# Two attentions in pairs of heads: another order of scores, minima and value projection, and a mixture product in banks of its own

## The chip, the cores and the metric

The kernel runs on one core of a Trainium2 chip. The metric is the device time of one execution in microseconds (us); of several executions the median counts. Five engines work side by side, each through its own instructions in order: TensorE (PE, with PEld for its weight loads), VectorE (DVE), ScalarE (ACT), GpSimd (POOL) and SyncE (SP), which here starts the DMAs. They wait for one another by semaphores.

## The reference, cut to what matters

The program is a chain of eight networks on 256 rows of 768 numbers. The change touches the first feed-forward network (`L0_ffn`, in the kernel `f0`) and the last one (`L3_ffn`, in the kernel `f3`). Both have an attention of 12 heads of width 64 over the 256 rows.

```python
# L0_ffn: x is (1, 256, 768)
normed = _ln(hidden_states, g1, b1)
scores = sigmoid(einsum('bld,d->bl', normed, Wr) + br)
_, idx = top_k(-scores, k)                      # k = 38 rows
attn_mask = zeros((b, l), bool).at[..., idx].set(True)
q, kk, v = (normed @ W + bias for q, k, v), 12 heads of 64
probs = softmax(einsum('blhd,bmhd->bhlm', q, kk) / sqrt(64), axis=-1)
attn_out = einsum('bhlm,bmhd->blhd', probs, v).reshape(b, l, d) @ Wo + bo
pooled = einsum('bl,bld->bd', scores / (sum(scores) + 1e-6), normed)
mix_out = (normed + scores[..., None] * pooled[:, None, :]) @ Wm + bm
merged = where(attn_mask[..., None], attn_out, mix_out)
h = hidden_states + merged                      # then a layer norm and a small gelu network

# L3_ffn: queries, keys and values with a low-rank part, then the same attention
attn = softmax(einsum('bhqd,bhkd->bhqk', q, k) * scale, axis=-1)
out = einsum('bhqk,bhkd->bhqd', attn, v) @ W_proj.T + b_proj
```

## The kernel before

Products are made at the precision of float32 by three products each: every weight tile of 128x768 is split by ScalarE into an upper part `WH` (line 294, `feed_act`) and by VectorE into a lower part `WL` (line 301, `feed_vec`), and activations are split the same way (lines 481 and 485: `act_upper`, `vec_lower`). There are four slots for split tiles, so `ahead(t)` feeds up to four tiles past t, and a slot is free when TensorE has done the product of the tile that held it. Each engine's program is written out by hand; no scheduler moves anything.

The attention goes by six pairs of heads, i = 0 to 5. `pair_scores` makes the scores of a pair (eight matmul records, line 358) in PSUM banks 0 and 1 or 2 and 3. VectorE takes their minima (the query is scaled by a negative number, so the minimum stands for the maximum) in `pair_least`, line 1367. ScalarE makes the exponentials with their row sums in `pair_exp`, line 1336. TensorE turns the exponentials (`turn_p`, eight transposes, line 363); ScalarE copies one half out of PSUM and VectorE the other (lines 474 and 477). VectorE makes the reciprocals of the row sums (line 1386) and, in the first network, multiplies them by the attention mask (line 1389); TensorE spreads them as rows (`spread`, line 1303). `mix` (line 1315) multiplies by the values in bank 6, `ctx` (line 1378) scales the result, and `upper` and `lower` split it for the output product.

Before: the minima of pair i+2 are the last step but one in VectorE's round i, behind the reciprocals, the lower part of pair i-2 and the copy; on TensorE the scores of pair i+2 come behind transposes and spreading of pair i. The whole value projection comes ahead of the loop.

In the first network the mixture's input `mixT` is masked on GpSimd (`l0ffn_pool`, line 1674) by a row that TensorE makes from the mask, and its lower part is made there too (line 1676). Behind the loop the mixture product and the attention's output product are summed in the same banks, for three blocks of 256 columns: each takes two tiles of one weight and then two of the other.

## Time and profile before

| | us |
|---|---|
| median of 3 runs | 1440.65 (1436.98 to 1444.83) |
| the profiled execution | 1440.82 |
| its span | 1439.0 |
| TensorE busy | 1347.7 |
| VectorE busy | 971.6 |
| ScalarE busy | 774.6 |
| GpSimd busy | 207.2 |

The span is the time from the first to the last recorded instruction; what the profiled execution took more, 1.8 us, lies around it. The engines overlap, so busy times don't add up to the span. The first network's part that matters lies from 547 to 624 us, the last network's from 1380 to 1435. In a timeline a row is a run of alike instructions with its start, its length, and in brackets how long the engine was idle before it and who ended that. PEclk is the granted share of TensorE's full clock (2.4 GHz; half of it is 1.2 GHz).

### The profile page before, as it was taken

To read this page: it belongs to the slowest core of one execution; us is meant where nothing else is said; L and a number is where in the kernel's file an instruction comes from. 1 tells how busy PE (TensorE), PEld (TensorE's weight loads), DVE (VectorE), ACT (ScalarE), POOL (GpSimd) and SP (SyncE) were. 2 spreads that over 40 slices of the span, in tenths; PEclk is the share of its full clock that TensorE was granted. 3 is DMA by queue.
4 is the path that set the end of the run, shared out by engine and by line. 5 is a ranking of instruction groups with operands and counts; after the bars stand their busy time and mean duration, and the time that the engine had idled before them with its cause. 6 is when DMAs were issued, how large, how long until landed. Compare 5 with 4: busy or idle time off the path is not lost.

```text
span 1439.0 us, 24211 instructions
## 1 busy us (share of the span) xinstructions
PE 1347.7 (94%) x10108; PEld 1157.6 (80%) x10108; DVE 971.6 (68%) x1708; ACT 774.6 (54%) x1260; POOL 207.2 (14%) x103
## 2 busy tenths in 40 slices
PE   9999999999999799888799999789999999998898
PEld 8999533799633588687688999769899999987786
DVE  8745777745777767566677767776677767768454
ACT  3445888545788545454545554634445544436344
POOL 0110776100677200002001000001000000000100
PEclk9999999999999999999899999899999999999899
DMA  9456364135464213035233453064355555232200
GB/s 355 111 201 189 100 181 121 67 132 170 128 197 121 76 68 121 1 139 202 99 136 142 171 180 132 23 242 132 134 187 176 169 194 192 73 152 102 77 1 23
DMA packets 30836, 194.82 MB, mean 135 GB/s; under 512 B 4212, under 2 KB 4340, under 8 KB 14727
## 3 DMA queue, kind: packets, MB, share of 16 engines
q1 hardware_dynamic: 30726, 193.27, 39.6%
q8 instruction: 80, 1.31, 0.4%
q14 instruction: 30, 0.24, 0.1%
HBM read 183.03 MB, written 3.93 MB: 130 GB/s over the span
## 4 chain that ended last, share of the span: by engine, by line
PE 73%; DVE 15%; ACT 7%; POOL 3%; issue 2%; DMA 0%; DVEq 0%; SPq 0%; ACTq 0%
PE PS L358 56%; PE PS L978 6%; PE PS L987 5%; DVE WL L301 3%; PE PS L363 3%; POOL WK L1173 2%; PE PS L619 1%; PE PS L460 1%; POOL WL L308 1%; DVE WK L1790 1%; ACT WK L1765 1%; ACT WH L294 1%; DVE WK L1795 1%; ACT WK L1336 1%; DVE SM L535 1%
## 5 line engine op out<-in xcount | busy, mean ns | idle before, releaser
L301 DVE TENSOR_TENSOR WL<-w,WH 128x768 fp32r<-128x768 f32 x373 | 355.6, 965 | 205.9 <-ACT WH L294 203.2
L294 ACT ACTIVATE WH<-w 128x768 fp32r<-128x768 f32 x381 | 315.4, 840 | 256.5 <-PE PS L358 243.0
L358 PE MATMUL PS<-XS,WH 128*128 128x256 f32 x2292 | 422.3, 287 | 14.2 <-DVE XS L485 7.1
L358 PEld LDWEIGHTS PS<-XS,WH 128*128 128x128 f32 x2292 | 359.5, 192 | 18.5 <-issue 11.1
L358 PE MATMUL PS<-XS,WL 128*128 128x256 f32 x1146 | 326.2, 285 | 0.0
L358 PEld LDWEIGHTS PS<-XS,WL 128*128 128x128 f32 x1146 | 220.1, 192 | 0.0
L1111 DVE TENSOR_TENSOR WK<-PS,WK 128x1024 f32<-128x1024 f32 x128 | 156.6, 1223 | 55.5 <-ACT PS L1055 54.5
L1173 POOL TENSOR_TENSOR WK<-WK 128x1024 f32<-128x1024 f32 x64 | 152.6, 2387 | 207.8 <-ACT WK L1052 207.8
L358 PE MATMUL PS<-WH,GS 128*128 128x256 f32 x864 | 159.6, 283 | 4.6 <-issue 1.4
L1055 ACT ACTIVATE PS<-PS 128x1024 f32<-128x1024 f32 x128 | 129.4, 1011 | 34.3 <-PE PS L978 34.2
L358 PEld LDWEIGHTS PS<-WH,GS 128*128 128x128 f32 x864 | 134.6, 188 | 7.7 <-issue 4.5
L978 PE MATMUL PS<-RT,PK 128*128 128x512 f32 x384 | 122.6, 427 | 0.2
L358 PE MATMUL PS<-WL,GS 128*128 128x256 f32 x432 | 121.6, 281 | 0.0
L978 PEld LDWEIGHTS PS<-RT,PK 128*128 128x128 f32 x384 | 62.3, 188 | 71.3 <-DVE WK L1111 54.0
L358 PE MATMUL PS<-WH,XS 128*128 128x256 f32 x552 | 109.6, 285 | 1.8 <-DVE XS L485 1.8
L1962 POOL TENSOR_TENSOR XT<-XS 128x512 f32<-128x512 f32 x9 | 13.5, 1525 | 665.9 <-DVE XS L485 665.9
L987 PE MATMUL PS<-WK,cp 128*32 128x384 f32 x1024 | 107.9, 497 | 1.5 <-POOL WK L1173 1.4
L358 PEld LDWEIGHTS PS<-WH,XS 128*128 128x128 f32 x552 | 88.1, 188 | 4.4 <-issue 3.3
L358 PEld LDWEIGHTS PS<-WL,GS 128*128 128x128 f32 x432 | 81.3, 188 | 0.0
L363 PE MATMUL PS<-cp,WK 128*128 128x128 f32 x332 | 56.0, 304 | 24.6 <-ACT WK L1765 9.4
L363 PEld LDWEIGHTS PS<-cp,WK 128*128 128x128 f32 x332 | 40.8, 154 | 44.3 <-ACT WK L1765 11.4
L358 PE MATMUL PS<-WK 64*128 64x256 f32 (+4 forms) x356 | 69.4, 373 | 3.0 <-ACT WK L474 2.3
(265 smaller groups left out, 2013.0 us busy)
## 6 DMA issues: line engine op xcount, KB each, us to landing
w<-f2W_in SPq DMA_DIRECT2D x40, 1152.0 KB, 5.4
w<-Wrel_in SPq DMA_DIRECT2D x12, 1152.0 KB, 7.5
WK<-qrep_in SPq DMA_DIRECT2D x16, 768.0 KB, 5.6
w<-f1Wi_in SPq DMA_DIRECT2D x8, 1152.0 KB, 5.3
w<-f1Wo_in SPq DMA_DIRECT2D x8, 1152.0 KB, 5.4
w<-f3Wqkv_in SPq DMA_DIRECT2D x6, 1152.0 KB, 15.1
RT<-qg_rows SPq DMA_DIRECT2D x16, 384.0 KB, 6.4
RT<-AS SPq DMA_DIRECT2D x32, 192.0 KB, 6.7
```

The costliest lines, as they stand in the source:

```text
L294: A.e.activation(w_hi(i), w_raw(i), ACT.Copy).then_inc(*hi("w", i))
L301: V.e.tensor_tensor(w_lo(i), w_raw(i), w_hi(i), ALU.subtract).then_inc(*lo("w", i))
L308: G.e.tensor_tensor(w_lo(i), w_raw(i), w_hi(i), ALU.subtract).then_inc(*log("w", i))
L358: ins = T.e.matmul(o, l, r, start=i == 0 and first, stop=i == n - 1 and last, skip_group_check=lint)
L363: return T.e.transpose(o, i, ident[0:n, 0:n])
L460: ins = T.e.matmul(b[:, 0:256], ident, iota[:, 0:256], start=True, stop=True)
L535: V.e.bn_stats(sm((name, "st", m), 18)[:, 6 * c:6 * c + 6], x3[:, m, 256 * c:256 * (c + 1)]).then_inc(*vec())
L978: ins = T.e.matmul(o, PK[:, j * P:(j + 1) * P], GR[b % 2][:, c:c + 512], start=True, stop=True)
L987: ins = T.e.matmul(o[32 * g:32 * (g + 1), 0:384], zsum[:, 28 - 4 * j:60 - 4 * j], SG[p % NSG][:, u, 384 * g:384 * (g + 1)], start=j == 0, ...
L1055: A.e.activation(SP[q], SP[q], ACT.Sigmoid).then_inc(*act("sig" + n, p, q))
L1111: V.e.tensor_tensor(SG[p % NSG][:, q // 2, 0:1024], SP[q], GQ[p // 4 % 2][:, 0:1024], ALU.mult).then_inc(*vec("prod" + n, p, q))
L1173: G.e.tensor_tensor(s, s, GQ[p // 4 % 2][:, 1024:1536].unsqueeze(1).broadcast_to((P, 2, 512)), ALU.mult).then_inc(*pool("prod" + n, p, 1))
```

## The change

In both attentions: TensorE makes the first two thirds of the value projection, then the scores of pair 2 and the transposes of pair 0, then the last third (`rest_v`), and then spreads pair 0. In a round i from 1 on the scores of pair i+2 come first, then transposes, spreading and the mix of pair i-1. VectorE takes the minima of pair i+2 first in its round, then its copy (`pair_out`), the reciprocals (`shares`), `lower` and `ctx`. ScalarE copies, makes the exponentials of pair i+2 and then copies the spread rows. The row sums have three buffers.

In the first network: GpSimd has no part in it any more. ScalarE and VectorE split the unmasked mixture ahead of the loop. Its product with `Wm` has banks of its own (`omB`): columns 0 to 255 behind the mix in round 4, 256 to 511 in round 5, and the last third behind the loop. VectorE multiplies the result by the mask as it adds it (`mixed_out`), and adds the attention's product (`omA`) to that (`om_out`). The weights lie in DRAM as six tiles of one and six of the other, and the third and fourth are split at the end of round 2 (`beside`). The row `g1be2` is loaded after the last output product. The ranking of rows is spread otherwise over VectorE's key projection.

```diff
         def pair_pe(...)
-            for i in range(6):
+            pair_scores(a, 2, qTv, kTv, free)
+            turn_p(0)
+            rest_v()
+            spread(0)
+            for i in range(1, 6):
+                if i + 2 < 6:
+                    pair_scores(a, i + 2, qTv, kTv, free)
                 turn_p(i)
                 spread(i)
-                if i + 2 < 6:
-                    pair_scores(a, i + 2, qTv, kTv, free)
-                if i:
-                    mix(i - 1)
+                mix(i - 1)
+                beside(i)
             mix(5)
...
         def pair_vec(...)
-            for i in range(6):
...
-                if i >= 2:
-                    lower(i - 2)
...
-                if i + 2 < 6:
-                    pair_least(a, i + 2)
-                if i:
-                    ctx(i - 1)
+            shares(0)
+            for i in range(1, 6):
+                if i + 2 < 6:
+                    pair_least(a, i + 2)
+                pair_out(a, i)
+                shares(i)
                 if i >= 2:
                     lower(i - 2)
+                ctx(i - 1)
+                beside(i)
...
         def l0ffn_pe():
+            def beside(i):
+                if i == 4:
+                    mixed(0, 0)
+                elif i == 5:
+                    mixed(256, 0)
+            pair_pe(att0, f0qA, f0kA, f0vA, there, rest_v, beside)
...
+            mixed(512, 2)
+            T.wait_ge(*row_sem("f0bom"))
+            for c in range(0, 768, 256):
+                om("omA", fom + 6, c, 4 if c < 512 else 6, xs_at, ...)
...
         def l0ffn_act():
+            pair_copy(att0, 0)
+            pair_exp(att0, 2)
             def beside(i):
                 if i == 2:
-                    A.wait_ge(pool, "mix")
-                    act_upper(GSv[:, 0, :, :], mixT, "mix")
+                    feed_act(ahead(fom))
...
         def l0ffn_vec():
+            def beside(i):
+                if i == 2:
+                    feed_vec(ahead(fom))
+            pair_vec(att0, beside, mkv[:, :, 0:1])
+            feed_vec(ahead(fom + 2))
+            mixed_out(0, 512)
+            feed_vec(ahead(fom + 4))
+            mixed_out(512, 768)
...
-        def l0ffn_pool():
-            G.e.tensor_tensor(mixT, mixT, mrow..., ALU.mult)
-            G.e.tensor_tensor(GSv[:, 1, :, :], mixT, GSv[:, 0, :, :], ALU.subtract)
```

The order of instructions shows the three places. First TensorE in the first network's pair loop, before: L363 transposes, L1303 spreading, L358 scores, L1315 mix.

```order
1733 L363 MATMUL PS<-cp,WK 128x128 x8
1734 L1303 MATMUL PS<-cp,SM 64x128 x4
1735 L358 MATMUL PS<-WK 128x256 x4
1736 L1315 MATMUL PS<-WK 64x256 x4
1737 L363 MATMUL PS<-cp,WK 128x128 x8
1738 L1303 MATMUL PS<-cp,SM 64x128 x4
```

And with the change:

```order
1732 L358 MATMUL PS<-WK 128x256 x4
1733 L363 MATMUL PS<-cp,WK 128x128 x8
1734 L1303 MATMUL PS<-cp,SM 64x128 x4
1735 L1315 MATMUL PS<-WK 64x256 x4
1736 L358 MATMUL PS<-WK 128x256 x4
1737 L363 MATMUL PS<-cp,WK 128x128 x8
```

The scores of the pair after next stood between spreading and mix; now they open the round, ahead of the transposes.

VectorE in rounds 2 and 3 of the same loop, before: L1367 is the minima, L1378 `ctx`, L1386 and L1389 reciprocal and mask, L485 a lower part, L477 the copy.

```order
343 L1367 TENSOR_REDUCE SM<-PS 128x4
344 L1378 TENSOR_TENSOR AhT<-PS,AhT 128x256
345 L1386 RECIPROCAL SM<-SM 128x4
346 L1389 TENSOR_TENSOR SM<-SM 128x4
347 L485 TENSOR_TENSOR XS<-AhT,XS 128x256
348 L477 COPY WK<-PS 128x512
349 L1367 TENSOR_REDUCE SM<-PS 128x4
350 L1378 TENSOR_TENSOR AhT<-PS,AhT 128x256
```

With the change (L1382 minima, L1398 and L1401 reciprocal and mask, L1409 `ctx`, L301 the lower parts of weight tiles):

```order
353 L1382 TENSOR_REDUCE SM<-PS 128x4
354 L477 COPY WK<-PS 128x512
355 L1398 RECIPROCAL SM<-SM 128x4
356 L1401 TENSOR_TENSOR SM<-SM 128x4
357 L485 TENSOR_TENSOR XS<-AhT,XS 128x256
358 L1409 TENSOR_TENSOR AhT<-PS,AhT 128x256
359 L301 TENSOR_TENSOR WL<-w,WH 128x768 x2
360 L1382 TENSOR_REDUCE SM<-PS 128x4
361 L477 COPY PK_<-PS 128x512
362 L1398 RECIPROCAL SM<-SM 128x4
363 L1401 TENSOR_TENSOR SM<-SM 128x4
```

Minima and copy stood behind the reciprocal and now stand ahead of it, and the lower parts of two weight tiles lie between the rounds.

ScalarE at the end of the loop, before: L1336 exponentials, L474 copies, L481 an upper part, L294 the upper parts of weight tiles.

```order
309 L1336 ACTIVATE WK,SM<-PS,SM 128x256 x4
310 L481 ACTIVATE XS<-AhT 128x256
311 L474 ACTIVATE WK<-PS 128x512
312 L474 ACTIVATE AhT<-PS 128x256
313 L481 ACTIVATE XS<-AhT 128x256
314 L474 ACTIVATE PK_<-PS 128x512
315 L474 ACTIVATE AhT<-PS 128x256
316 L481 ACTIVATE XS<-AhT 128x256 x2
317 L294 ACTIVATE WH<-w 128x768 x12
```

With the change (L1344 exponentials):

```order
309 L1344 ACTIVATE WK,SM<-PS,SM 128x256 x4
310 L474 ACTIVATE AhT<-PS 128x256
311 L481 ACTIVATE XS<-AhT 128x256
312 L474 ACTIVATE WK<-PS 128x512
313 L474 ACTIVATE AhT<-PS 128x256
314 L481 ACTIVATE XS<-AhT 128x256
315 L474 ACTIVATE PK_<-PS 128x512
316 L474 ACTIVATE AhT<-PS 128x256
317 L481 ACTIVATE XS<-AhT 128x256 x2
318 L294 ACTIVATE WH<-w 128x768 x10
```

The feeding of weights, from the fifth tile of the mixture's weight on now, still begins only behind the last upper part of the loop.

## Rows read from the trace of the kernel before

**Rows 1.** The page: TensorE's busy time, the chain by engine, a costly group.

```profile
PE 1347.7 (94%) x10108; PEld 1157.6 (80%) x10108; DVE 971.6 (68%) x1708; ACT 774.6 (54%) x1260; POOL 207.2 (14%) x103
...
PE 73%; DVE 15%; ACT 7%; POOL 3%; issue 2%; DMA 0%; DVEq 0%; SPq 0%; ACTq 0%
...
L301 DVE TENSOR_TENSOR WL<-w,WH 128x768 fp32r<-128x768 f32 x373 | 355.6, 965 | 205.9 <-ACT WH L294 203.2
```

**Rows 2.** Stretches: us, busy of PE, PEld, DVE, ACT, POOL; then granted clock, DMA.

```profile
547.40:624.10 76.70, 69.79 (x538) 58.04 (x537) 44.76 (x70) 36.72 (x89) 6.86 (x2) 0.96 0.17 55
568.00:572.00 4.00, 4.00 (x24) 2.98 (x24) 2.06 (x4) 1.61 (x6) 0.00 (x0) 0.58 0.00 0
1397.90:1421.60 23.70, 20.21 (x177) 13.48 (x177) 13.19 (x27) 14.35 (x49) 0.00 (x0) 1.00 0.00 1
1415.00:1418.00 3.00, 2.16 (x21) 1.50 (x22) 1.15 (x3) 2.58 (x11) 0.00 (x0) 1.00 0.00 0
```

**Rows 3.** Timeline of TensorE, first network: start, length, instructions, idle before.

```profile
567.40 0.66 PE L1303 MATMUL PS<-cp,SM 128*64 128x128 f32 x8 [2.43 <-DVE SM L1389]
...
569.40 1.97 PE L363 MATMUL PS<-cp,WK 128*128 128x128 f32 x8
...
586.42 1.12 PE L1303 MATMUL PS<-cp,SM 128*64 128x128 f32 x8 [2.04 <-ACT WK L474]
...
593.26 0.38 PE L358 MATMUL PS<-WH,GS 128*128 128x256 f32 x1
```

**Rows 4.** Timeline of VectorE, first network.

```profile
563.94 3.40 DVE L1389 TENSOR_TENSOR SM<-SM 128x4 f32<-128x4 f32 x1
...
584.01 2.26 DVE L1389 TENSOR_TENSOR SM<-SM 128x4 f32<-128x4 f32 x1
...
624.08 0.42 DVE L1649 TENSOR_TENSOR WK<-PS,XN 128x256 f32<-128x256 f32 x1 [1.37 <-PE PS L358]
```

**Rows 5.** Timeline of GpSimd, first network.

```profile
563.90 3.43 POOL L1674 TENSOR_TENSOR WK<-WK 128x1536 f32<-128x1536 f32 x1 [84.97 <-DVE SM L1386]
582.82 3.43 POOL L1676 TENSOR_TENSOR GS<-WK,GS 128x1536 fp32r<-128x1536 f32 x1 [15.49 <-ACT GS L481]
```

**Rows 6.** Timeline of TensorE, last network.

```profile
1399.42 0.66 PE L1303 MATMUL PS<-cp,SM 128*64 128x128 f32 x8
1400.00 1.13 PE L358 MATMUL PS<-WK 64*128 64x256 f32 x8
1401.07 1.09 PE L363 MATMUL PS<-cp,WK 128*128 128x128 f32 x8
1402.64 0.66 PE L1303 MATMUL PS<-cp,SM 128*64 128x128 f32 x8 [0.48 <-DVE SM L1386]
...
1407.98 1.08 PE L1315 MATMUL PS<-WK 128*64 128x256 f32 x8
1409.00 1.09 PE L363 MATMUL PS<-cp,WK 128*128 128x128 f32 x8
```

**Rows 7.** Timeline of VectorE, last network.

```profile
1401.19 1.22 DVE L1367 TENSOR_REDUCE SM<-PS 128x4 f32<-128x1024 f32 x1 [0.97 <-PE PS L358]
...
1408.28 0.68 DVE L477 COPY WK<-PS 128x512 f32<-128x512 f32 x1
1408.88 1.21 DVE L1367 TENSOR_REDUCE SM<-PS 128x4 f32<-128x1024 f32 x1
1410.01 0.41 DVE L1378 TENSOR_TENSOR WK<-PS,WK 128x256 f32<-128x256 f32 x1
1410.34 0.17 DVE L1386 RECIPROCAL SM<-SM 128x4 f32<-128x4 f32 x1
```

**Rows 8.** Timeline of ScalarE, first network.

```profile
576.49 0.42 ACT L481 ACTIVATE XS<-AhT 128x256 fp32r<-128x256 f32 x1
...
594.16 1.56 ACT L294 ACTIVATE WH<-w 128x768 fp32r<-128x768 f32 x2
...
643.83 0.85 ACT L294 ACTIVATE WH<-w 128x768 fp32r<-128x768 f32 x1 [1.50 <-PE PS L358]
```

More of the change, by code:

```diff
@@ L1368, in pair_least, with pair_out, pair_vec, shares @@
                               ALU.min).then_inc(*vec(a.name + "least", i))
-        def pair_vec(a, keep=None):
+        def pair_out(a, i):
             n = a.name
+            V.wait_ge(pe, n + "tp", i, 1)
+            if i >= 2:
+                V.wait_ge(pe, n + "mix", i - 2)
+            vec_copy(a.PT[i % 2][:, 1, :, :], two(ps(n + "tp", i, 1)), n + "pt", i)
+        def pair_vec(a, beside, keep=None):
+            n = a.name
+            def shares(i):
+                r = a.rs[i % 3]
+                V.wait_ge(act, n + "E", i, 1, 1)
+                V.e.reciprocal(r, r).then_inc(*vec())
+                if keep is not None:
+                    V.wait_ge(vec)
+                    V.e.tensor_tensor(r, r, keep.broadcast_to((P, 2, 2)), ALU.mult).then_inc(*vec())
+                vec.also(n + "rs", i)
             def ctx(i):
@@ L1546, in l0ffn_act @@
             fetch("f0exp", ACT.Exp)
+            for k in range(0, 6, 2):
+                A.wait_ge(vec, "mixT", k + 1)
+                act_upper(pair_of(GSv, 0, k), mixT[:, k:k + 2, :], "mix", k)
             for i in range(2):
@@ L1598, in l0ffn_vec, with rank @@
             V.e.tensor_copy(scol, ps("scol")[:, 0:256:128]).then_inc(*vec("scol"))
-            for m in range(2):
-                vec_gemm(fk, 2 * m + 2, None, 2 * m)
+            def rank(m):
                 sc = scol[:, m:m + 1]
@@ L1611, in l0ffn_vec @@
                 V.e.tensor_reduce(rk[:, m:m + 1], Gt, AX.X, ALU.add).then_inc(*vec())
+            rank(0)
+            for f in range(6):
+                vec_gemm(fk, f + 1, None, f)
+                V.wait_ge(vec, "pooled")
+                V.e.scalar_tensor_tensor(out=mixT[:, f, :], in0=srow, scalar=pooled[:, f:f + 1], in1=nT[:, f, :],
+                                         op0=ALU.mult, op1=ALU.add).then_inc(*vec("mixT", f))
+            rank(1)
             mkv = mk2.rearrange("p (m a) -> p m a", m=2)
@@ L1627, in v_out @@
                                       ALU.add).then_inc(*vec("f0v", c0, m))
+            pair_least(att0, 0)
             feed_vec(ahead(fv))
-            pair_least(att0, 0)
             pair_least(att0, 1)
-            V.wait_ge(pe, "mrow")
-            V.e.tensor_copy(mrow, ps("mrow")[:, 0:256]).then_inc(*vec("mrow"))
+            for k in range(0, 6, 2):
+                vec_lower(pair_of(GSv, 1, k), mixT[:, k:k + 2, :], pair_of(GSv, 0, k), "mix", k)
+            feed_vec(ahead(fv + 2))
+            v_out(0, 512)
@@ new lines, in l0ffn_vec, with mixed_out @@
+            pair_least(att0, 2)
+            feed_vec(ahead(fv + 4))
+            pair_out(att0, 0)
+            v_out(512, 768)
+            def beside(i):
+                if i == 2:
+                    feed_vec(ahead(fom))
+            pair_vec(att0, beside, mkv[:, :, 0:1])
+            def mixed_out(c0, c1):
+                for m in range(2):
+                    V.wait_ge(pe, "omB", c1 - 256, m)
+                    V.e.scalar_tensor_tensor(out=hx[:, m, c0:c1], in0=n_out("omB", c0, c1, m), scalar=mkv[:, m, 1:2],
+                                             in1=xn3[:, m, c0:c1], op0=ALU.mult, op1=ALU.add).then_inc(*vec("hxB", c0, m))
@@ L1634, in l0ffn_vec, with om_out @@
+            def om_out(c0, c1):
+                for m in range(2):
+                    V.wait_ge(pe, "omA", c1 - 256, m)
+                    V.wait_ge(vec, "hxB", c0, m)
+                    V.e.tensor_tensor(hx[:, m, c0:c1], hx[:, m, c0:c1], n_out("omA", c0, c1, m),
+                                      ALU.add).then_inc(*vec("hx", c0, m))
+            feed_vec(ahead(fom + 2))
             V.wait_ge(pe, "mT")
             V.e.tensor_copy(mT[0:2, :], ps("mT")[0:2, 0:256]).then_inc(*vec("mT"))
-            feed_vec(ahead(fv + 2))
@@ L1977, in l1gnn_sync @@
             load_row("g1br2", 768, (vec, "f0v", 512, 1))
[L1978 removed]
+            load_row("g1be2", 768, (pe, "omA", 512, 1))
             load_units(w1 + 10)
```

178 lines of the change are left out of this document (75 added, 103 removed).

## The prediction

> **What bounds the kernel now.** I read the page first. TensorE is busy 94% of the span and 73% of the chain that ended last is TensorE work [rows 1], so a change pays only where TensorE waits or its clock is low, and costs wherever it makes TensorE wait. Then I asked for the busy time of the two stretches that the change touches. From the end of the first network's key projection to its last output product there are 76.7 us with 69.8 us of TensorE work, so 6.9 us of waiting, at a mean granted clock of 0.96 [rows 2]. In the last network, from the end of the value projection to the last mix, there are 23.7 us with 20.2 us of work: 3.5 us of waiting, clock 1.00 [rows 2]. That bounds the gain: 6.9 us of waits, some 3 us of low clock ((1 - 0.96) x 76.7) and 3.5 us, 13.4 us in all. The clock loss has two places: after a wait of 2.43 us the eight transposes took 1.97 us instead of 1.09, and after one of 2.04 us the eight row products took 1.12 instead of 0.66 [rows 3, 6]; the granted clock behind the first was 0.58 [rows 2]. The reader should see the cause of both in the next groups: VectorE's multiply of a 128x4 tile took 3.40 us and later 2.26 us, where a reciprocal of that shape takes 0.17 [rows 7], exactly while GpSimd ran its two operations of 3.43 us [rows 4, 5].
>
> **Part one, what goes.** The masking on GpSimd goes, and with it both stalls. Left alone this would take away nearly all of the 2.43 and 2.04 us waits and the 3 us of low clock behind them. Two transposes for the mask row go as well (0.3 us at 1.02 us for eight), and half of the last value block's time is used: scores of pair 2 and the first transposes run before its 256 last columns.
>
> **Part two, the new order in a round of the pair loop.** This is where I think the change loses. Durations and pitches are from the last network, which no GpSimd disturbs [rows 6, 7]: eight score products are 1.07 us on TensorE, eight transposes 1.02, eight row products 0.58, the mix 1.02; on VectorE the minima hold the queue 1.13 us, the copy 0.60, the context product 0.33, the reciprocal is 0.17, and the row products start 0.15 us after it.
> Before, a round's row products waited only for a reciprocal that stood ahead of the copy and of the next minima. Now TensorE does scores(i+2), transposes(i), row products(i), mix(i-1), and VectorE does minima(i+2), copy(i), reciprocal(i). So the row products wait for a chain that starts when the scores end: 0.11 us to VectorE (tail of the last product and signal), 1.13 + 0.60 + 0.17 + 0.15 = 2.16 us. Only the transposes, 1.02 us, run meanwhile. TensorE waits 1.14 us in each of rounds 1, 2 and 3. In rounds 4 and 5 there are no minima, but the copy needs the transposes: 0.11 + 0.60 + 0.17 + 0.15 = 1.03 us. Round 0 has its reciprocal behind the last value evacuation: 0.11 + 0.34 + 0.17 + 0.06 = 0.68 us. The last mix still waits for its single bank, some 0.55 us. Sum for the last network: 0.68 + 3.42 + 2.06 + 0.55 = 6.7 us of waits, where there are 3.5 us now: **+3.2 us**. Its work is unchanged, and the output projection still follows directly.
>
> **Part three, the first network.** Each round has one more small VectorE operation (the keep multiply, 0.2 us), so rounds 1 and 2 wait 1.35 us, rounds 4 and 5 1.23 us, round 0 0.88 us. Two places are worse.
> Round 3: the feeding of two weight tiles now stands at the end of round 2, on ScalarE (two tiles 1.56 us [rows 8]) and on VectorE ahead of the minima of pair 5 (0.97 us for one [rows 1]). The chain from the end of mix(1): 0.11, context product 0.41, signal 0.04, its upper part on ScalarE 0.34 [rows 8], two tiles 1.56, signal 0.04, second lower tile 0.88 in the queue, minima 1.13, copy 0.60, reciprocal and keep 0.37, 0.15: 5.6 us. TensorE has the scores of pair 5 and the transposes of pair 3 for it, 2.1 us. It waits 3.5 us.
> The third mixture block: it needs tiles 5 and 6 of that matrix, and ScalarE can split them only after the loop's last step, since its queue is in order. From the end of mix(5): 0.11 + 0.41 + 0.04 + 0.34 + 1.56 + 0.04 + 0.96 + 0.06 = 3.5 us, less 0.5 us for the little transposing product that stands between: 3.0 us of waiting. Before, tiles for the first 5.9 us of the output product were ready at that point, and the product (593.26 to 624.08, 30.8 us [rows 3, 4]) ran on without a wait; its work only moves. The rest of it I cost at nothing: the extra VectorE additions (four, about 2.2 us) lie beside TensorE's products of 36 matmuls, and the later weight tiles are split a block ahead. The g1be2 row load now waits for the last product and has the next weights behind it on the SP queue, some 5 us later relative to the work; ScalarE first takes those weights at 643.83, 19.8 us after that product [rows 4, 8], so I cost it at nothing too.
> Waits of the first network: 0.88 + 2.70 + 3.5 + 2.46 + 3.0 + 0.1 = 12.6 us. Do the two mixture blocks placed in rounds 4 and 5 fill waits? By the order, no: they stand after the mix, and each round's wait lies between transposes and row products.
> Clock: waits of 2.43 and 2.04 us were each followed by a fall to half, 1.2 GHz, and cost 1.57 and 1.33 us (each group's excess over its usual duration). The new waits of 3.5 and 3.0 us are longer; bounds are 0 and 1.7 us each (the larger of the two with a small margin), and I take 1.5 us each, since both rows lie near it: 3.0 us. The waits of 1.1 to 1.35 us in rounds of 5 us I cost at nothing: the last network was busy 2.16 of 3.0 us in a stretch at clock 1.00 [rows 2], about the new share.
> Sum: work at full clock 69.8 - 3.0 - 0.3 = 66.5 us, waits 12.6, low clock 3.0: 82.1 us against 76.7: **+5.4 us**.
>
> **The number.** The profiled execution took 1440.8 us beside a span of 1439.0 and a median of 1440.65, so it is a typical one. 1440.8 + 3.2 + 5.4 = 1449.4 us. Neither sum is more exact than about 1 us, since each rests on some ten signal times.
>
> **The rivals.**
> A. The clock holds through both long waits. For it: the two blocks beside them are dense work, and where a fall comes depends on what surrounds a wait. Against it: both shorter waits of before had a fall. It gives 1446.4 us. This is the case that ends on the other side, not slower by a measurable amount; it decides from a fall that costs less than about 0.7 us each.
> B. The waits are filled after all: the mixture blocks let ScalarE and VectorE run ahead by a pair, and with GpSimd gone the loops run without a gap over 0.5 us. Then the first network is 66.5 + 3 = 69.5 us (-7.2) and the last one stays: 1433.6 us. It needs round i's reciprocal to be done before its transposes, which the order on VectorE excludes for rounds 1 to 3.
> C. The pair loops run at half clock throughout. The eight transposes took 1.97 us then against 1.09, so a round's 3.7 us of work become some 6.7; 0.9 of that hides in the wait. Eight rounds of the two networks by 2.1 us, less the 3 us already counted: 1463 us. Against it: clock 1.00 in the stretch cited above. The Trainium skill, "TensorE: Matmul & The Clock Gate", Part 4, says that transposes don't count as busy time for the clock; by that rule the new rounds would be busy for little over half of their time, and C would be the likely case. The trace does not bear it out: a third of the matrix work in that stretch of the last network is transposes.
> D. The rounds are shorter than summed, since signals overlap with work, and the loss is about half: 1445 us.
>
> **How the numbers follow.** Forecast, with one or both falls of the clock, 55%; A 24%; D 8%; B 6%; C 7%. A measurement here can tell about 0.5%, 7.2 us, from no change: that is 1433.4 to 1447.9 us. A and D lie inside it, and so do some of the forecast's own outcomes (a part of them without the full price): I give them 2 of its 55. Slower: 53 + 7 = 60%; same: 24 + 8 + 2 = 34%; faster: 6%. The range runs from 1444.0 (D with a margin for a run's spread) to 1453.0 (the sum with both falls at 1.7 us and 0.2 us more in each round), and leaves out B and C.
>
> **What would show it.** Right: in the last network, waits of 1.0 to 1.2 us before the row products of rounds 1 to 5, put down to VectorE; in the first, one of about 3.5 us before those of round 3 and one of about 3 us ahead of the third mixture block, put down to VectorE's lower tile; a granted clock well under 1 behind each; no GpSimd work there, and every keep multiply at 0.2 us. Wrong: gaps under 0.7 us in rounds 1 to 3, or a row-product group that starts straight after its transposes; then the order on VectorE does not hold it up as I think. If both stretches measure as summed and the time still differs, something behind them moved, for which I have no term.

## The result, and the profile after

The changed kernel took 1444.15 us, the median of 19 runs (1439.41 to 1447.29); the kernel before, run beside it, took 1438.35 us (median of 19, 1433.58 to 1444.83). The ratio is 1.0038, with a 95% interval of 1.0027 to 1.0048: slower by 5.5 us, between 3.9 and 6.9. The terms of the forecast added up to +8.6 us. The direction and the places of the waits were right, the size was not, and the difference is small enough to lie within what the prediction had called no change. The time itself, 1444.15 us, lies 0.15 us above the lower edge of the forecast's range.

The page of the changed kernel, first its size, TensorE's busy time and the chain by engine:

```profile
span 1443.0 us, 24234 instructions
...
PE 1342.9 (93%) x10106; PEld 1155.2 (80%) x10106; DVE 969.6 (67%) x1714; ACT 776.5 (54%) x1262; POOL 200.2 (14%) x101
...
PE 73%; DVE 16%; ACT 6%; POOL 3%; issue 2%; DMA 0%; DVEq 0%; SPq 0%; ACTq 0%
```

Beside [rows 1]: in these two traces TensorE was busy for 4.8 us less and the span is 4.0 us longer. So the loss is waiting, and VectorE has one more hundredth of the chain.

The two stretches, with the same columns as [rows 2]. The first network's runs from the first scores to the second layer norm's first statistics; the last network's from the first low-rank products of its value projection to VectorE's last addition behind the output projection, which contains all that the change touches there. A short window behind a wait stands between them.

```profile
548.20:628.10 79.90, 67.53 (x535) 57.82 (x534) 43.52 (x78) 37.25 (x91) 0.00 (x0) 0.98 0.12 40
604.00:608.00 4.00, 3.41 (x17) 3.41 (x18) 3.91 (x6) 0.88 (x2) 0.00 (x0) 0.57 0.00 0
1386.00:1438.70 52.70, 46.23 (x388) 39.45 (x386) 25.36 (x45) 23.98 (x68) 0.00 (x0) 1.00 0.00 1
```

The same stretch of the last network in the kernel before:

```profile
1384.40:1434.70 50.30, 46.75 (x388) 39.16 (x386) 25.18 (x44) 24.14 (x72) 0.00 (x0) 1.00 0.00 1
```

In the first network GpSimd is gone (0.00) where it had 6.86 us [rows 2]. In the last one the stretch is 2.3 us longer although the busy time of TensorE fell from 46.75 to 46.23 us: waiting went from about 3.5 to about 6.4 us.

Timeline of TensorE, changed kernel, first network: the row products (L1303) that waited, and the third mixture block's first product (L358), as [rows 3] show them for before:

```profile
570.25 0.66 PE L1303 MATMUL PS<-cp,SM 128*64 128x128 f32 x8 [1.27 <-DVE SM L1401]
...
575.13 0.66 PE L1303 MATMUL PS<-cp,SM 128*64 128x128 f32 x8 [1.27 <-DVE SM L1401]
...
582.32 0.66 PE L1303 MATMUL PS<-cp,SM 128*64 128x128 f32 x8 [3.58 <-DVE SM L1401]
...
586.02 0.66 PE L1303 MATMUL PS<-cp,SM 128*64 128x128 f32 x8 [1.16 <-DVE SM L1401]
...
604.59 0.58 PE L358 MATMUL PS<-WH,GS 128*128 128x256 f32 x1 [3.04 <-DVE WL L301]
```

With round 0 (0.89) and round 5 (1.16) the first network's waits are 12.4 us. What VectorE does ahead of the longest of them, in its own timeline (against [rows 4]):

```profile
578.33 1.83 DVE L301 TENSOR_TENSOR WL<-w,WH 128x768 fp32r<-128x768 f32 x2 [1.22 <-ACT WH L294]
580.07 1.22 DVE L1382 TENSOR_REDUCE SM<-PS 128x4 f32<-128x1024 f32 x1
581.21 0.68 DVE L477 COPY PK_<-PS 128x512 f32<-128x512 f32 x1
581.81 0.17 DVE L1398 RECIPROCAL SM<-SM 128x4 f32<-128x4 f32 x1
582.01 0.16 DVE L1401 TENSOR_TENSOR SM<-SM 128x4 f32<-128x4 f32 x1
```

Two weight tiles, then the minima, then the copy, and only then the reciprocal and the keep multiply, each under 0.2 us, that TensorE waits for. The keep multiply L1401 takes 0.16 us, where L1389 took 3.40 and 2.26 us [rows 4].

Timeline of TensorE, changed kernel, last network, beside [rows 6]:

```profile
1395.35 1.09 PE L363 MATMUL PS<-cp,WK 128*128 128x128 f32 x8
1396.20 0.36 PE L358 MATMUL PS<-WH,XS 128*128 128x256 f32 x1
...
1406.08 0.66 PE L1303 MATMUL PS<-cp,SM 128*64 128x128 f32 x8 [1.07 <-DVE SM L1398]
1406.54 1.06 PE L1315 MATMUL PS<-WK 128*64 128x256 f32 x8
...
1415.45 0.66 PE L1303 MATMUL PS<-cp,SM 128*64 128x128 f32 x8 [1.08 <-DVE SM L1398]
...
1418.96 0.66 PE L1303 MATMUL PS<-cp,SM 128*64 128x128 f32 x8 [0.96 <-DVE SM L1398]
```

Waits of about 1.1 us in the rounds with minima and 0.96 us in those without. One detail is new: the mix starts 0.46 us after the row products, where in [rows 6] the scores started 0.58 us after them; and the value block starts 0.85 us after the first transposes.

### The profile page after: what moved, and what is told of

It is laid out like the page before. It is cut to its first block, busy times and chain, and to the rows that moved or that the text cites. A ratio compares the mean times of both kernels' runs of the same rounds, so it can differ in the third digit from the quotient of the medians.

```text
span 1443.0 us, 24234 instructions
## 1 busy us (share of the span) xinstructions
PE 1342.9 (93%) x10106; PEld 1155.2 (80%) x10106; DVE 969.6 (67%) x1714; ACT 776.5 (54%) x1262; POOL 200.2 (14%) x101
## 4 chain that ended last, share of the span: by engine, by line
PE 73%; DVE 16%; ACT 6%; POOL 3%; issue 2%; DMA 0%; DVEq 0%; SPq 0%; ACTq 0%
PE PS L358 56%; PE PS L978 6%; PE PS L987 5%; DVE WL L301 3%; PE PS L363 3%; POOL WK L1173 2%; PE PS L619 2%; PE PS L460 1%; POOL WL L308 1%; ACT WH L294 1%; DVE WK L1833 1%; ACT WK L1808 1%; DVE WK L1838 1%; PE PS L1315 1%; DVE SM L535 1%
## 5 line engine op out<-in xcount | busy, mean ns | idle before, releaser
L301 DVE TENSOR_TENSOR WL<-w,WH 128x768 fp32r<-128x768 f32 x373 | 354.6, 962 | 194.6 <-ACT WH L294 192.0
L294 ACT ACTIVATE WH<-w 128x768 fp32r<-128x768 f32 x381 | 315.5, 840 | 252.9 <-PE PS L358 239.1
L358 PE MATMUL PS<-XS,WH 128*128 128x256 f32 x2292 | 420.3, 286 | 14.2 <-DVE XS L485 7.1
L358 PEld LDWEIGHTS PS<-XS,WH 128*128 128x128 f32 x2292 | 357.9, 191 | 18.6 <-issue 11.2
L358 PE MATMUL PS<-XS,WL 128*128 128x256 f32 x1146 | 325.4, 284 | 0.0
L358 PEld LDWEIGHTS PS<-XS,WL 128*128 128x128 f32 x1146 | 218.9, 191 | 0.0
L358 PE MATMUL PS<-WH,GS 128*128 128x256 f32 x864 | 161.6, 285 | 7.7 <-DVE WL L301 3.9
L358 PEld LDWEIGHTS PS<-WH,GS 128*128 128x128 f32 x864 | 136.5, 191 | 10.7 <-issue 4.2
L358 PE MATMUL PS<-WL,GS 128*128 128x256 f32 x432 | 122.7, 284 | 0.0
L358 PE MATMUL PS<-WH,XS 128*128 128x256 f32 x552 | 110.5, 285 | 2.3 <-DVE XS L485 2.3
L358 PEld LDWEIGHTS PS<-WH,XS 128*128 128x128 f32 x552 | 88.4, 188 | 5.5 <-issue 5.4
L358 PEld LDWEIGHTS PS<-WL,GS 128*128 128x128 f32 x432 | 82.7, 191 | 0.0
L363 PE MATMUL PS<-cp,WK 128*128 128x128 f32 x332 | 54.8, 299 | 22.0 <-ACT WK L1808 9.4
L363 PEld LDWEIGHTS PS<-cp,WK 128*128 128x128 f32 x332 | 40.0, 151 | 39.9 <-ACT WK L1808 11.3
L358 PE MATMUL PS<-WK 128*128 128x64 f32 (+4 forms) x356 | 69.1, 372 | 3.1 <-ACT WK L474 2.3
```

Of the source, the lines that this page charges most:

```text
L294: A.e.activation(w_hi(i), w_raw(i), ACT.Copy).then_inc(*hi("w", i))
L301: V.e.tensor_tensor(w_lo(i), w_raw(i), w_hi(i), ALU.subtract).then_inc(*lo("w", i))
L358: ins = T.e.matmul(o, l, r, start=i == 0 and first, stop=i == n - 1 and last, skip_group_check=lint)
L363: return T.e.transpose(o, i, ident[0:n, 0:n])
```

## The experiments

**Theory.** The loss is the order in VectorE's round (minima and copy ahead of the reciprocal that TensorE waits for) and two places where weight tiles are split at the wrong moment; the removal of GpSimd's part is a gain that these eat up. **Rival 1:** the waits come from the longer chain as such, the scores that now open the round, and go with no reordering on VectorE. **Rival 2:** the price is the clock that falls behind the waits. **Rival 3:** something behind the stretches moved.

A comparison by medians is uncertain by one to three microseconds here, so each kernel was also read by stretches of its trace. Here is what every execution that was traced gave, with borders set at the same instructions in each (us; "ahead" and "middle" are code that no kernel changed; the last columns are the mean granted clock and TensorE's busy time in the first network's stretch, the latter to about 0.1 us):

```
kernel              ahead  first net  middle  last net   tail    span   clock, busy
before             547.47      76.95  759.99     50.30   4.29  1439.0   0.96, 69.99
before_again       545.80      78.27  756.77     50.30   4.36  1435.5   0.93, 71.39
e6_last_only       545.50      78.21  760.15     52.60   4.34  1440.8   0.93, 71.28
e5_no_gpsimd       548.25      71.68  758.54     50.30   4.33  1433.1   1.00, 67.64
after              548.25      80.17  757.61     52.60   4.37  1443.0   0.98, 67.83
after_again        548.27      83.00  754.25     52.60   4.38  1442.5   0.94, 70.63
after_third        546.75      81.58  758.65     52.60   4.32  1443.9   0.96, 69.13
e9_filled_waits    548.50      78.71  757.96     52.60   4.33  1442.1   1.00, 72.24
e1_recip_first     548.26      74.67  759.29     47.24   4.34  1433.8   0.98, 67.65
e2_feed_round5     545.84      75.88  758.12     52.60   4.36  1436.8   1.00, 66.58
e3_feed_round4     548.31      76.47  757.44     52.60   4.28  1439.1   1.00, 66.45
e4_all_three       545.94      67.18  756.08     47.24   4.36  1420.8   1.00, 66.24
e8_all_and_first   545.55      66.81  750.76     47.06   4.32  1414.5   1.00, 66.31
```

The last network's stretch is the same to the digit wherever its code is the same. The first network's is not: 80.17, 83.00 and 81.58 us for the changed kernel, 76.95, 78.27 and 78.21 us for the old code. Its means are 81.6 and 77.8 us: +3.8 us, and with +2.3 us in the last network 6.1 us, inside the interval of the ratio.

### The reciprocals first: e1_recip_first

The changed kernel with the reciprocals (and the keep multiply) first in VectorE's round, in both networks.

```diff
             for i in range(1, 6):
+                shares(i)
                 if i + 2 < 6:
                     pair_least(a, i + 2)
                 pair_out(a, i)
-                shares(i)
```

> The changed kernel with one edit: in both attentions VectorE's round begins with the reciprocals (shares), then minima, copy, lower, ctx. Theory (the new waits come from VectorE's order, since minima and copy stand between the scores and the reciprocal): the waits before the row products of rounds 1 to 5 vanish in the last network (1.07, 1.08, 1.08, 0.96, 0.96 us, together 5.15 us) and in rounds 1, 2, 4 and 5 of the first (4.86 us); round 3 of the first keeps part of its 3.58 us (the tiles still stand ahead, about 1.9 us left). Together about -11.5 us against the changed kernel, so some 6 us below the kernel before. Rival (the round is bound by the exponentials or the copy behind them anyway): the waits come back before the transposes or the mix, and the gain is under 4 us.

Measured: 1433.57 us, ratio to before 0.9975 (0.9961 to 0.9989). By the ratios that is 3.6 us below before (by the medians 5.2) and 9 us below the changed kernel; the two stretches are 12.3 us shorter than the changed kernel's means, where 11.5 were expected. The two stretches, first and last network:

```profile
548.30:622.90 74.60, 67.65 (x535) 57.82 (x535) 43.65 (x78) 36.90 (x91) 0.00 (x0) 0.98 0.13 43
...
1382.20:1429.50 47.30, 45.93 (x388) 38.98 (x386) 25.39 (x45) 23.59 (x68) 0.00 (x0) 1.00 0.01 1
```

And the one long wait left in its pair loop, the row products of round 3 in TensorE's timeline:

```profile
578.34 0.66 PE L1303 MATMUL PS<-cp,SM 128*64 128x128 f32 x8 [2.28 <-DVE SM L1401]
```

The last network went from 52.60 to 47.24 us: its waits of 6.4 us became 1.4 us, and it is now 3.1 us shorter than before the change. Rival 1 falls: the scores still open the round, and the waits are gone. What stays in round 3 is the two weight tiles that stand ahead of the reciprocal: 2.28 us, where 1.9 were expected.

### The weight tiles: e2_feed_round5 and e3_feed_round4

e2 adds the feeding of the next two tiles at the end of round 5, so that they are there for the third mixture block. e3 moves the feeding of round 2 to round 4. Both change ScalarE's and VectorE's side alike.

```diff
e2
             def beside(i):
                 if i == 2:
                     feed_act(ahead(fom))
+                elif i == 5:
+                    feed_act(ahead(fom + 2))
...
e3
             def beside(i):
-                if i == 2:
+                if i == 4:
                     feed_act(ahead(fom))
```

> The changed kernel with one edit: ScalarE and VectorE split the fifth and sixth tile of the mixture's weight at the end of round 5 and not behind the loop. Theory: the 3.04 us wait ahead of the third mixture block vanishes and with it the fall of the clock behind it (1.5 us): -4.5 us against the changed kernel. Rival (the loop's last step is late whatever is fed): the two tiles push copy, upper and lower of the last pairs back and TensorE waits the same time before the attention's output product: 0 us.

> The changed kernel with one edit: the third and fourth tile of the mixture's weight are split at the end of round 4, beside the first mixture block, and not at the end of round 2. Theory: the wait of 3.58 us in round 3 falls to 1.27 us as in rounds 1 and 2: -2.3 us. Rival (the second mixture block then waits for its tiles, or the wait only moves to round 4): 0 us or slower.

Measured: e2 1442.52 us, ratio 1.0026 (1.0008 to 1.0044); e3 1442.90 us, ratio 1.0016 (0.9998 to 1.0033). Both intervals touch the changed kernel's, so the medians alone don't decide. The stretches do. e2, first network:

```profile
545.80:621.70 75.90, 66.58 (x535) 56.83 (x535) 43.56 (x78) 37.26 (x91) 0.00 (x0) 1.00 0.13 43
```

e3, the same stretch, and in TensorE's timeline its row products of round 3 and the third mixture block:

```profile
548.30:624.80 76.50, 66.45 (x535) 56.75 (x535) 43.83 (x79) 37.37 (x91) 0.00 (x0) 1.00 0.12 42
...
580.07 0.66 PE L1303 MATMUL PS<-cp,SM 128*64 128x128 f32 x8 [1.28 <-DVE SM L1401]
...
602.34 0.39 PE L358 MATMUL PS<-WH,GS 128*128 128x256 f32 x1 [3.04 <-DVE WL L301]
```

In e2 the wait of 3.04 us is gone. The stretch is 75.88 us against 81.6: 3.0 us is the wait, and the other 2.7 us is the clock, which did not fall in this execution, not even behind the wait of 3.58 us in round 3, which e2 still has. The 4.5 us that were expected count a part of that clock; the median is only 1.7 us lower by the ratios. In e3 the wait of 3.58 us became 1.28, like its neighbours, and the other stayed at 3.04. Its stretch, 76.47 us, is 5.1 us shorter, of which 2.3 us is the wait and the rest the clock, which did not fall in this execution although the second wait is still there. Both waits that the prediction put down to the tiles are where it put them; what their removal saves in clock can't be told from one trace each.

### All three: e4_all_three

The edits of e1, e2 and e3 together.

```diff
             for i in range(1, 6):
+                shares(i)
                 if i + 2 < 6:
                     pair_least(a, i + 2)
                 pair_out(a, i)
-                shares(i)
...
             def beside(i):
-                if i == 2:
+                if i == 4:
                     feed_act(ahead(fom))
+                elif i == 5:
+                    feed_act(ahead(fom + 2))
```

> The changed kernel with the three edits of the runs before together. Theory: the waits of the first network's stretch fall from 12.4 us to about 1.5 us and the clock stays up (1.5 us), those of the last from about 6.4 to 1.2 us: -17 us against the changed kernel, about 1.2% below it and some 0.8% below the kernel before. Rival (another engine bounds the rounds at about 4.4 us each, as in the kernel before): half of it.

Measured: 1423.21 us, ratio 0.9903 (0.9883 to 0.9922). Its two stretches:

```profile
545.90:613.10 67.20, 66.24 (x535) 56.34 (x535) 43.63 (x78) 37.01 (x91) 0.00 (x0) 1.00 0.14 48
...
1369.20:1416.40 47.20, 45.91 (x388) 38.97 (x386) 25.32 (x44) 23.57 (x68) 0.00 (x0) 1.00 0.00 1
```

1.0 and 1.3 us of waiting are left. The stretches are 14.4 and 5.4 us shorter than the changed kernel's, 19.8 us in all, where the medians (by their ratios to before) differ by 19.4. Of the 14.4 us, 11.4 are waits, and about 2.7 are clock, which stayed up in this trace. The loss is explained, and this version beats both kernels: by the ratios 14 us below before and 19 us below the changed one. What moved behind the stretches (rival 3) is no cause of the loss: in the table the tail is 4.28 to 4.38 us in every trace, and the middle has a mean of 759.0 us in the three traces with the old code in the first network and 756.8 us in those of the changed kernel, so it is if anything shorter.

### One part alone: e5_no_gpsimd and e6_last_only

e5 is the kernel before with GpSimd's part gone: ScalarE and VectorE split the mixture ahead of the loop, and the masking of the mixture is left out. The order in the rounds, the shared banks and the weights' order stay as they were.

```diff
-            G.e.tensor_tensor(mixT, mixT, mrow..., ALU.mult)
-            G.e.tensor_tensor(GSv[:, 1, :, :], mixT, GSv[:, 0, :, :], ALU.subtract)
...
         def l0ffn_vec():
+            for k in range(0, 6, 2):
+                vec_lower(pair_of(GSv, 1, k), mixT[:, k:k + 2, :], pair_of(GSv, 0, k), "mix", k)
```

> The kernel before with only the GpSimd part taken out: the mixture is split ahead of the loop on ScalarE and VectorE as in the changed kernel, and not masked (the mask on the mixture's input is left out, so rows under the mask get both products); rounds, banks and weight order stay as before. Theory (the stalls of VectorE came from GpSimd's two operations, and the falls of the clock from the waits they made): the keep multiply takes 0.2 us in every round, the waits of 2.43 and 2.04 us shrink to under 0.9 us, the clock stays at 1.00 in the stretch: -6 us against the kernel before. Rival (the waits have another cause, such as the copies on ScalarE, and the stalls were only beside them): -1 to -2 us.

Measured: 1432.22 us, ratio 0.9960 (0.9942 to 0.9977), 5.8 us faster than before. Its first network, and in TensorE's timeline the row products of rounds 0, 1 and 4; those of rounds 0 and 4 had waited 2.43 and 2.04 us [rows 3]:

```profile
548.20:619.90 71.70, 67.64 (x539) 56.70 (x538) 41.22 (x73) 36.65 (x91) 0.00 (x0) 1.00 0.17 59
...
566.29 0.66 PE L1303 MATMUL PS<-cp,SM 128*64 128x128 f32 x8
...
569.71 0.66 PE L1303 MATMUL PS<-cp,SM 128*64 128x128 f32 x8 [0.67 <-DVE SM L1389]
...
582.39 0.66 PE L1303 MATMUL PS<-cp,SM 128*64 128x128 f32 x8 [0.71 <-DVE SM L1389]
```

The wait of round 0 is gone, that of round 4 is 0.71 us, and round 1, which had none, now has 0.67. The keep multiply of round 0, which had 3.40 us, in VectorE's timeline:

```profile
565.33 0.16 DVE L1389 TENSOR_TENSOR SM<-SM 128x4 f32<-128x4 f32 x1
```

So the change holds a gain of 6.1 us (71.68 against 77.8): 2.8 us less waiting, and 3.3 us of clock, which stayed at 1.00 in this one trace. All the rest of it in the first network costs 9.9 us (81.6 against 71.68).

e6 is the kernel before with the new order in the last network alone.

```diff
-            pe_gemm_N("f3v", zv, 6, 768, xs_at, ...)
-            pair_pe(att3, f3qA, f3kA, f3vA, there)
+            new_pair_pe(att3, f3qA, f3kA, f3vA, there, rest_v, beside)
```

> The kernel before with the new order (value projection in two parts, scores first, minima first on VectorE) in the last network only; the first network stays as it was. Theory: the stretch of the last network is 2.3 us longer, as in the changed kernel (52.6 against 50.3 us), so +2.3 us or 0.16% in all. Rival (its length depends on what ran before it): another length of that stretch.

Measured: 1438.70 us, ratio 1.0017 (0.9999 to 1.0035), so +2.4 us with an interval from 0 to 5; the trace is more exact:

```profile
545.50:623.70 78.20, 71.28 (x538) 59.14 (x538) 45.01 (x70) 36.75 (x89) 6.86 (x2) 0.93 0.16 55
...
1383.90:1436.50 52.60, 46.16 (x388) 39.37 (x386) 25.26 (x45) 23.90 (x68) 0.00 (x0) 1.00 0.00 1
```

The last network's stretch is that of the changed kernel, 52.60 us, and the first one is like before.

### The same kernels again: after_again, after_third, before_again

One more traced execution each, of the changed kernel twice and of the old one once.

> The changed kernel again, unchanged, for its trace. Whether the clock falls behind the waits of 3.58 and 3.04 us of the first network: if it is set by the order of work, it is as in the first trace, no fall behind 3.58 us and one behind 3.04 us (stretch 80.2 us); if it depends on where a wait lies in time, either can differ, and the stretch is 78.7 us with no fall or up to 81.7 with two.

> The changed kernel, unchanged, a third trace: the waits as in the first two (12.4 us in the first network's stretch), the stretch anywhere from 78.6 to 83.0 us, by the clock.

> The kernel before, unchanged, for a trace of its own. The waits of 2.43 and 2.04 us of the first network are there; the stretch has 66.9 us of work at full clock and 6.9 us of waits. If the falls of the clock are a matter of where the waits lie in time, it has another length than 76.95 us, between 74 and 79 us; if they are set by the order of work, 76.95 us again.

Measured: 1444.27, 1445.72 and 1437.26 us. after_again, first network, two windows in it, and in TensorE's timeline the row products of rounds 3 and 4:

```profile
548.30:631.30 83.00, 70.63 (x535) 60.12 (x535) 43.80 (x79) 37.34 (x91) 0.00 (x0) 0.94 0.12 39
584.00:588.00 4.00, 2.84 (x18) 2.47 (x20) 1.64 (x5) 1.01 (x2) 0.00 (x0) 0.50 0.00 0
608.00:612.00 4.00, 4.00 (x25) 4.00 (x24) 3.06 (x5) 0.00 (x0) 0.00 (x0) 0.63 0.00 0
...
582.33 0.66 PE L1303 MATMUL PS<-cp,SM 128*64 128x128 f32 x8 [3.57 <-DVE SM L1401]
...
586.96 1.12 PE L1303 MATMUL PS<-cp,SM 128*64 128x128 f32 x8 [1.16 <-DVE SM L1401]
```

The same wait, 3.57 us here and 3.58 in the first trace, was followed by half clock here (0.50; the row products of round 4 took 1.12 instead of 0.66 us) and by none there. The price can be read from the distances between the starts of the same instructions. From the row products of round 3 to the third mixture block they are 22.3 us in the first trace, 24.9 here and 23.6 in after_third: the clock behind the first wait cost 0, 2.7 and 1.3 us. From there to the end of the stretch they are 23.8, 24.0 and 23.9 us against 22.4 in e3, where the clock held: 1.4, 1.6 and 1.5 us behind the second. before_again, first network:

```profile
545.80:624.10 78.30, 71.39 (x538) 59.25 (x538) 45.06 (x71) 36.75 (x89) 6.86 (x2) 0.93 0.16 55
```

With the borders of the table that is 1.3 us longer than in the first trace (78.27 against 76.95); the busy time is longer by the same amount and the waits are the same 6.9 us, so it is clock.

### The clock: e9_filled_waits

The changed kernel with useless products in the two long waits, seven ahead of the row products of round 3 and six ahead of the third mixture block, so that TensorE is not idle there.

```diff
         def spread(i):
             b = bank_at(7, (n + "rb", i), (act, n + "rb", i))
+            if n == "f0" and i == 3:
+                for _ in range(7):
+                    T.e.matmul(b[:, 0:256], ident, iota[:, 0:256], start=True, stop=True, ...)
             T.wait_ge(vec, n + "rs", i)
```

> The changed kernel with matmuls of no use in its two long waits: seven ahead of the row products of round 3 in the first network, six ahead of the third mixture block (each 0.44 us by its pitch, so 3.1 and 2.6 us), into banks that are overwritten behind them. They take nothing from the path, since TensorE waited there. Theory (part of what the first network loses is the clock behind these waits, and it differs between executions): the stretch has clock 1.00 and is 78.6 us, against 80.2 and 83.0 us in the two traces of the changed kernel; the median falls by 1.5 to 4.5 us. Rival (the clock costs nothing on the whole, as it falls elsewhere in its place): the median stays.

Measured: 1443.25 us (nine runs, 1435.83 to 1446.53), ratio 1.0037 (1.0010 to 1.0063). First network, and in TensorE's timeline the filling and what it left of the waits:

```profile
548.50:627.20 78.70, 72.24 (x561) 61.40 (x561) 43.69 (x78) 37.23 (x91) 0.00 (x0) 1.00 0.12 41
...
578.82 3.19 PE L1303 MATMUL PS<-cp 128*128 128x256 f32 x14
582.47 0.66 PE L1307 MATMUL PS<-cp,SM 128*64 128x128 f32 x8 [0.46 <-DVE SM L1405]
...
604.76 0.39 PE L359 MATMUL PS<-WH,GS 128*128 128x256 f32 x1 [0.25 <-DVE WL L302]
```

In the trace it did what was meant: clock 1.00 throughout, 78.71 us, 2.9 us below the mean of the changed kernel, which is the clock's part. The median does not show it; the interval (1.0010 to 1.0063 against 1.0038) would allow 4.0 us less than the changed kernel as well as 3.6 us more. Rival 2 is so answered only in part: within the first network's stretch the clock costs 1.3 to 4.1 us in the traces of the changed kernel and 2.4 to 3.8 us in those of the old code, so it is no source of the loss, which is in the waits (6.9 us in the old code's traces, 12.4 in each of the changed kernel's); whether keeping it up saves anything over the whole program is left open.

### Pair 0 too: e8_all_and_first

e4 with pair 0's reciprocals ahead of VectorE's copy for that pair and of its last addition for the value projection.

```diff
         def pair_vec(...)
-            shares(0)
...
+            pair_shares(att0, 0, mkv[:, :, 0:1])
...
+            pair_shares(att3, 0)
```

> The kernel with all three edits (e4_all_three) and one more: the reciprocals of pair 0 stand ahead of its copy and of the last value evacuation. Theory: the only waits over 0.6 us that are left, 0.89 us in the first network and 0.69 us in the last ahead of pair 0's row products, vanish: -1.5 us against e4_all_three, stretches of 66.3 and 46.6 us. Rival (the mix of pair 0 then waits for the value evacuation instead): half of that or nothing.

Measured: 1427.53 us (six runs, 1416.30 to 1428.76), ratio 0.9921 (0.9895 to 0.9948). The row products of pair 0 in TensorE's timeline:

```profile
563.16 0.66 PE L1303 MATMUL PS<-cp,SM 128*64 128x128 f32 x8 [0.52 <-DVE WK L1663]
```

VectorE's timeline, the reciprocals of pair 0 and the last addition of the value projection:

```profile
560.27 0.17 DVE L1396 RECIPROCAL SM<-SM 128x4 f32<-128x4 f32 x1
...
562.68 0.42 DVE L1663 TENSOR_TENSOR WK<-PS,r 128x256 f32<-128x256 f32 x1 [1.11 <-PE PS L358]
```

The reciprocals are done 2.7 us early, and TensorE still waits 0.52 us: bank 7, into which the row products go, holds the last block of the value projection, and that must be added first. The stretches are 0.37 and 0.18 us shorter than in e4; medians of e4 and e8 can't be told apart. The expectation took the reciprocal for the only holder and was a miss by most of its size.

## Why the prediction was right or wrong, point by point

**The cause, in both networks: right.** The waits summed and measured, in us:

| | summed | measured |
|---|---|---|
| first network, round 0 | 0.88 | 0.89 |
| rounds 1 and 2 | 1.35 each | 1.27, 1.27 |
| round 3 | 3.5 | 3.58 |
| rounds 4 and 5 | 1.23 each | 1.16, 1.16 |
| third mixture block | 3.0 | 3.04 |
| all of the first network | 12.6 | 12.4 |
| all of the last network | 6.7 | 6.4 |

Each is put down to the engine and line named, and in e1 to e4 all but two go by the edit that their cause asks for: round 0's, 0.89 and 0.69 us, and the 0.52 us ahead of the last mix stay. For round 0 the prediction named the reciprocal alone; e8 shows that the bank holds it too, with 0.52 us left in either network. In parts two and three the signal times added up well. One sign of part one came true only in part: with GpSimd's part gone and the old order kept (e5), the waits of 2.43 and 2.04 us became none and 0.71, but a new one of 0.67 us stands in round 1.

**The step that failed first: "Its work is unchanged".** The last network's work was counted as unchanged and the first one's as 0.3 us less. TensorE's busy time in the last network fell from 46.75 to 46.23 us, and in the first one, at clock 1.00 in both, from 67.64 us (e5, the old order) to 66.45 or 66.58 (e3 and e2): 1.1 us less. Together 1.6 us less where 0.3 were counted. Where it went can be read from the distances between starts, with the waits taken off. In the last network row products hold TensorE 0.46 us where the mix follows and 0.58 us where scores do [rows 6]; in rounds 1 to 3 the mix now follows, 3 x 0.12 = 0.36 us, and over all six rounds it is 0.42 us. The transposes hold it 0.16 us less (those of pair 0 0.85 us ahead of the value block, where a group ahead of row products held it 1.02), the mixes 0.10 us less, and the value projection with the scores, now in two pieces, 0.13 us more: 0.55 us by this count, 0.52 by the busy time. In the first network (e5 against e2) the row products, the transposes and the mixes hold it 0.40, 0.40 and 0.20 us less and the weight products 0.33 us more, and the two transposes of the mask, counted at 0.3 us, had held it 0.36: 1.0 of the 1.1 us. I had taken the old neighbourhood's durations for the new one.

**The second step: the last network's +3.2 us.** Its waits grew by 2.85 us (3.5 to 6.4), not 3.2, and less work took it to +2.3 us. e6 shows that number alone.

**The third step: the clock's price was taken as equal.** It was put at 3.0 us before and after. Measured as busy time less the work at full clock (67.6 us before, 66.5 after), it is 2.4, 3.8 and 3.7 us in the three traces with the old code, mean 3.3, and 1.3, 4.1 and 2.6 in those of the changed kernel, mean 2.7. The sum was well estimated, its parts were not: the bounds for one fall were 0 and 1.7 us, and behind the first wait it cost 0, 2.7 and 1.3 us. The difference of the means, 0.6 us, is smaller than the spread of either three, so it is no finding.

**The sum.** First network: work -1.1 us (counted -0.3), waits +5.5 (from 6.9 to 12.4; counted +5.7), clock -0.6 (counted 0): +3.8 us for +5.4. Last network: work -0.5 (counted 0), waits +2.85 (counted +3.2): +2.3 us for +3.2. Together +6.1 for +8.6; the ratio gives +5.5. More than half of the miss is the work term, 1.3 of 2.5 us. For the absolute time the start is the largest term: 1440.8 us was called typical on the strength of three runs, and over 19 runs the median of before is 1438.35. Of the 5.2 us between 1449.4 and 1444.15 that is 2.4. Some luck is in the first network's sum. It gave 82.1 us for the changed kernel, with 66.5 us of work, and the means are 81.6 and 66.5. But the 66.5 came from taking 3.0 us of clock off a trace that had 2.4, and 0.3 us of saved work where 1.1 were saved; the two errors cancel. What the forecast had too low there was the stretch of before: 76.95 us in the one trace that it had, 77.8 in the mean of three. The upper end of the range does not follow from what it says either: two falls at 1.7 us and 0.2 us more in each of twelve rounds give 1452.2, not 1453.0.

**The rivals.** A, the clock holds: it did behind the 3.58 us wait in one trace (and the kernel came out at 1444.2, below the 1446.4 of A), but in the next two it fell behind both. It is not one case or the other but a matter of the single execution. B, the waits are filled: refuted by every wait in the table. It is, though, what e4 makes true. C, half clock in the loops: the last network's stretch has clock 1.00 in every trace. D, the rounds are shorter than summed and half the loss comes, 1445 us: nearest in time, but not in its mechanism. The waits came nearly in full; it was the work that shrank. The half clock that the prediction named as a sign behind each long wait was there in five of six cases in the three traces of the changed kernel.

**Chances.** "Slower by over 0.5%" had 60%, "no change" 34%. +0.38% is no change by that bound. The forecast of 1449.4 us lay only 1.5 us above the bound of 1447.9, and the sum was called exact to about 1 us in each of two networks; so putting 53 of the forecast's 55% on the far side was too much.

## What to carry to other kernels

In an in-order queue ask of every operation that another engine waits for what stands ahead of it: here a 0.17 us reciprocal behind 1.7 us of minima and copy cost about 1.1 us in each round, and its move to the front, one line, turned a loss into a gain. A change that removes a real stall can still lose by what travels with it; trying its parts alone (e5: -6.1 us; the rest: +9.9 us) shows which to keep, and with the rest mended the kernel was 14 us faster than before. When pitches are taken from the trace, take them with the neighbour that the new order gives, and take the state of before from more than one execution.

## What the runs showed of the hardware

The stall of VectorE's small multiply under GpSimd's work is confirmed by its absence: 3.40 and 2.26 us with GpSimd's operations of 3.43 us beside it [rows 4, 5], 0.16 us in the same place without them (e5), where the stretch is 6.1 us shorter. The Trainium skill, "SBUF — State Buffer", section "SBUF: two separate sides", states the mechanism: the two engines share a pair of ports, and where a VectorE operation with two SBUF inputs meets a GpSimd operation that reads SBUF, the one that starts first has the pair for its whole instruction and the other blocks. The trace agrees: GpSimd's operation started first both times, and the multiply, which reads two SBUF tiles, ends 0.01 and 0.02 us after the GpSimd operation beside it (567.34 after 567.33, 586.27 after 586.25). VectorE's timeline of the kernel before also shows what is not held. These two ran at their usual length inside GpSimd's second operation (582.82 to 586.25 us); one reads PSUM and one SBUF tile, the other a single SBUF tile:

```profile
583.48 0.41 DVE L1378 TENSOR_TENSOR AhT<-PS,AhT 128x256 f32<-128x256 f32 x1
583.81 0.17 DVE L1386 RECIPROCAL SM<-SM 128x4 f32<-128x4 f32 x1
```

No run here varied the operands on purpose.

The granted clock after the same wait in the same kernel differs between executions: 3.58 us and no fall, 3.57 us and 0.50 in the window behind. Behind the 3.04 us wait it was 0.57 in one trace of the changed kernel (604 to 608 us), 0.63 in another (608 to 612), and 1.00 for the whole stretch in e3. Two shorter waits, 2.43 and 2.04 us, had each been followed by half clock in the trace of before.

The pair loop of the last network, in which eight of every 32 matmul records are transposes and TensorE waits 1 us of 5, stayed at clock 1.00 in every trace. The Trainium skill, "TensorE: Matmul & The Clock Gate", Part 4, says of transposes that they don't count as busy in the same way. By that rule one would have expected a fall that no run shows.

The unchanged middle of the program took from 750.8 to 760.2 us between traces, more than all that the change does. TensorE's busy time there, on 5319 to 5321 matmul records, runs from 688.5 to 700.8 us, and its waiting only from 59.4 to 62.4 us; between the two traces of the kernel before, 3.1 of the 3.2 us are busy time. So it is the pace of the same work that differs; the mean granted clock of the middle is 0.96 in twelve traces and 0.97 in the shortest (e8). What sets it stays open. It is why single runs of this kernel can't be compared below some 10 us, and why the stretches decided more than the medians did.
